# One row-maximum instruction for both heads of a softmax step, over a score tensor of two PSUM banks

## The reference, cut to what matters

```python
xn = layernorm(x)                                   # x: 8 batches x 512 rows x 256
out = x + attn(xn) + ffn(xn)
# attn: 16 heads of 16 channels, causal
score = Q @ K.T / 4 + mask
p = exp(score - max(score, axis=-1)); p = p / sum(p)
a = (p @ V) @ WO
# ffn: 16 heads of 64 channels, no mask, rotary q and k
p = softmax(q @ k.T / 8)
v = sum over the 2 chosen of 8 experts of gate * (x @ Wv[expert])
o = p @ v;  src2 = sum over the 2 chosen of 8 experts of gate * (o @ Wo[expert])
src = ln(x + src2);  ln(src + relu(src @ W1 + b1) @ W2 + b2)
```

## Time and profile before

| | |
|---|---|
| median of 3 runs | 3404.29 us (3403.39 to 3406.31) |
| span of the profiled execution | 3401.4 us |
| PE busy | 3233.1 us, 95% |
| DVE busy | 2439.7 us, 72% |
| ACT busy | 1961.5 us, 58% |
| POOL busy | 1441.9 us, 42% |
| row maxima (L1136) | 1024 instructions, 551.8 us busy |
| exponentials (L957) | 1024 instructions, 590.7 us busy |

### The profile page before, as it was taken

The page is one execution under the profiler, slowest core; times in us unless marked ns, Lnnn a source line. Parts: engine busy times, 40 slices in busy tenths (PEclk is TensorE's granted clock), DMA queues, the critical chain, the costliest instruction groups (busy, mean ns, idle before and its releaser), DMA issues.

```text
span 3401.4 us, 64468 instructions
## 1 busy us (share of the span) xinstructions
PE 3233.1 (95%) x18240; PEld 2378.9 (70%) x18240; DVE 2439.7 (72%) x4708; ACT 1961.5 (58%) x4509; POOL 1441.9 (42%) x1215
## 2 busy tenths in 40 slices
PE   1699999999999999999999999999999999997998
PEld 1577777777777777777777777777777777775765
DVE  6577777777777777777777777777777777775554
ACT  2466666656666666666666666666666666664121
POOL 4144355445443454345543554434534543442212
PEclk9999999999999999999999999999999999999999
DMA  5223333334233333233233332333332433333221
GB/s 165 76 71 87 95 90 85 77 76 109 76 84 87 84 98 81 75 100 96 69 87 76 96 98 77 76 104 81 84 87 68 114 81 75 84 75 110 72 83 62
DMA packets 115937, 295.18 MB, mean 87 GB/s; under 512 B 33856, under 2 KB 54592, under 8 KB 99264
## 3 DMA queue, kind: packets, MB, share of 16 engines
q1 hardware_dynamic: 115904, 294.78, 32.9%
HBM read 262.74 MB, written 31.98 MB: 87 GB/s over the span
## 4 chain that ended last, share of the span: by engine, by line
PE 85%; issue 6%; DVE 5%; ACT 3%; DMA 1%; POOL 0%; ACTq 0%; SPq 0%; DVEq 0%; POOLq 0%
PE bank L673 27%; PE bank L799 22%; PE bank L718 9%; PE bank L773 7%; PE bank L688 5%; PE bank L905 4%; PE bank L897 3%; PE bank L693 3%; PE bank L745 2%; PE bank L754 2%; ACT probs L957 2%; DVE uf L1239 1%; DVE oo L1232 1%; PE bank L694 1%; ACT pt_e L977 1%
## 5 line engine op out<-in xcount | busy, mean ns | idle before, releaser
L573 POOL TENSOR_TENSOR u_l<-uf,u_h 128x512 fp32r<-128x512 f32 x512 | 716.1, 1409 | 722.6 <-ACT u_h L1041 722.4
L1136 DVE TENSOR_REDUCE nmax<-bank 128x1 f32<-128x512 f32 (+3 forms) x1024 | 551.8, 579 | 305.0 <-PE bank L688 297.8
L673 PE MATMUL bank<-wv_h,xx 128*128 128x512 f32 x2048 | 755.0, 410 | 7.1 <-DVE vm L1157 7.1
L957 ACT ACTIVATE probs<-bank,nmax 128x512 f32<-128x512 f32 (+3 forms) x1024 | 590.7, 610 | 253.2 <-DVE nmax L1136 253.1
L1041 ACT ACTIVATE u_h<-uf 128x512 fp32r<-128x512 f32 x512 | 321.7, 632 | 696.9 <-DVE uf L1239 683.6
L673 PEld LDWEIGHTS bank<-wv_h,xx 128*128 128x128 f32 x2048 | 386.0, 188 | 155.8 <-issue 59.6
L718 PEld LDWEIGHTS bank<-ident_sb,probs 128*128 128x128 f32 x3328 | 388.3, 141 | 106.4 <-issue 51.3
L718 PE MATMUL bank<-ident_sb,probs 128*128 128x128 f32 x3328 | 451.3, 274 | 1.6 <-ACT stackT L1032 0.9
L569 POOL TENSOR_TENSOR v_sb<-v_next,zero_hb 128x512 f32<-128x512 f32 x64 | 74.2, 1160 | 891.9 <-PE bank L773 877.4
L799 PE MATMUL bank<-u_h,wo_h 128*128 128x512 f32 x1024 | 427.1, 417 | 5.0 <-ACT u_h L1041 3.2
L1239 DVE TENSOR_TENSOR uf<-oo,go 128x512 f32<-128x512 f32 x512 | 416.2, 823 | 8.8 <-POOL u_l L573 6.6
(11 more groups left out here) (141 smaller groups left out, 5164.2 us busy)
## 6 DMA issues: line engine op xcount, KB each, us to landing
go<-go_d SPq DMA_DIRECT2D x256, 512.0 KB, 6.5
xx<-xs_d SPq DMA_DIRECT2D x128, 512.0 KB, 3.5
oo<-scale_d SPq DMA_DIRECT2D x128, 128.0 KB, 2.9
a_d<-a_out SPq DMA_DIRECT2D x128, 128.0 KB, 2.3
pt_c<-in_x SPq DMA_DIRECT2D x16, 512.0 KB, 4.7
st<-in_wv SPq DMA_DIRECT2D x16, 512.0 KB, 5.8
st<-in_wo SPq DMA_DIRECT2D x16, 512.0 KB, 7.2
go_d<-go_turned SPq DMA_DIRECT2D x256, 8.0 KB
```

Of the source, the lines that this page charges most:

```text
L573: nc.gpsimd.tensor_tensor(u_l[:, e % 2], uf[:, e % 2], u_h.bitcast(f32)[:, e % 2], ALU.subtract).then_inc(ul_done, 1)
L673: last = nc.tensor.matmul(out, lhs, rhs, start=n == 1, stop=n == 3 * len(chunks))
L957: nc.scalar.activation(probs[:, s % 2, j, 0:w], sbank[j][:, 0:w], ACT.Exp, bias=nmax[:, 2 * s + j:2 * s + j + 1], **kw).then_inc(exp_done, 1)
L1136: nc.vector.tensor_reduce(nmax[:, 2 * s + j:2 * s + j + 1], sbank[j][:, 0:w], AX.X, ALU.max, negate=True).then_inc(nmax_ready, 1)
```

## The change

The two score banks become one tensor `score` of [128, 2, 512], that is two banks, and `sbank[j]` its halves; the other six banks are declared behind it (so the banks have other addresses, with the same use). A step's two row maxima, one for each head, become one instruction that reads both halves and writes two columns of `nmax`. It waits until the scores of both heads are complete; it raises `nmax_ready` once a step instead of twice, and ACT waits once a step, ahead of the exponential of head 0.

```diff
-        bank = [ctx.enter_context(nc.psum_tensor(f"bank{i}", [NP, S], f32)) for i in range(8)]
+        score = ctx.enter_context(nc.psum_tensor("score", [NP, 2, S], f32))
+        sbank = [score[:, j] for j in range(2)]
+        others = [ctx.enter_context(nc.psum_tensor(f"bank{i}", [NP, S], f32)) for i in range(6)]
+        bank = [o[:] for o in others[0:2]] + sbank + [o[:] for o in others[2:6]]
         ybank = bank[0:2]
-        sbank = bank[2:4]
...
                 for j in range(2):
-                    act.wait_ge(nmax_ready, n * UNITS + 2 * s + j + 1)
+                    if j == 0:
+                        act.wait_ge(nmax_ready, n * SLOTS + s + 1)
...
             def row_max(s, n):
 
                 w = S if s % 2 == 0 else (s // 2 + 1) * NP
-                for j in range(2):
-                    dve.wait_ge(s_full, n * UNITS + 2 * s + j + 1)
-                    nc.vector.tensor_reduce(nmax[:, 2 * s + j:2 * s + j + 1], sbank[j][:, 0:w], AX.X, ALU.max, negate=True).then_inc(nmax_ready, 1)
+                dve.wait_ge(s_full, n * UNITS + 2 * s + 2)
+                nc.vector.tensor_reduce(nmax[:, 2 * s:2 * s + 2], score[:, :, 0:w], AX.X, ALU.max, negate=True).then_inc(nmax_ready, 1)
```

## The result

The changed kernel takes 3459.73 us (3458.57 to 3461.42), against 3404.09 us before: 1.0161 times, 95% interval 1.0146 to 1.0175. It is slower, as forecast, and within 1 us of the forecast time. That closeness is luck: it hides three terms that were each off, one of them in its sign, and they happen to add up to the right sum. The profiled execution has a span of 3457.2 us, 55.8 more than before's.

What follows compares the result with a forecast made beforehand. PE, busy 95%, was taken as the bound, DVE counting only where PE waits. Delays of 0.37, 0.43 and 0.09 make 0.89 us a pair, x 63 = 56 us, so 3460 us, 1.65% slower; range 3431 to 3478.

Steps and rivals of the forecast that it cites:

- The estimate that the prediction made beside it: Joint 2 x 512 maximum on DVE: by the skill's 125 ns access overhead it would take 1.24 us, saving 0.125.
- Length of the instruction: Joint maximum of 2 x 512 columns on DVE: 1.22 us, between bounds of 1.216 and 1.36.
- Rival 2: The two-bank read saves nothing: joint maximum 1.36 us, exponentials 0.67 late, kernel 3482 us; chance 0.10.
- A: Step 5, maximum 6: late exponentials delay q_h and q_l, so V5's weight load starts 0.37 us later a pair.
- B: Step 7, next pair's maximum 0: late SO0 and SO1 copies hold turn(7)'s head 1 transposes, +0.43 us a pair.
- C: Step 2, maximum 3: exponentials 0.29 later delay UH2 and POOL's chain, so J3 loads +0.09 us later a pair.
- Only one of A and B: Rival: only one of the delays A and B bites, giving 3430 to 3436 us; chance 0.15.
- Faster: Rival: DVE's gain reaches PE, QK1's wait shortens by 0.07 us a pair, 3396 to 3400 us; chance 0.05.
- No change: Rival: ACT's waits take up the exponentials' delay and the gain is off the path, 3404 us; chance 0.07.

## Why the prediction was right, point by point

**The bound.** PE sets the pair and DVE's saved time counts only where PE waits for it: borne out. DVE's saving of 0.07 in a step of 512 columns is real (1.13 to 1.14 from a joint maximum's start to the next instruction's) and moved nothing at most places. The estimate that the prediction made beside it took the 0.125 of the Trainium skill, Perfetto Trace Analysis, Optimizing Scalar/DVE Operations, off the lengths of the profile's rows, while the page gives it as engine-busy time; what answers to that here is the distance from start to start, and one instruction less saved 0.07 of it.

**Length of the instruction:** 1.22 taken, 1.221 measured. Rival 2, no saving (1.36), falls with it.

**A, V5:** 0.37 forecast; 0.45 by the blocks, 0.44 by the pairs. Right mechanism, shown twice over, by the two instructions at step 6 and by the moved q_h. It was mis-sized for two small reasons. "Waiting for head 1's adds nothing" was off: the maximum starts 1.03 us after the scores' first load instead of 1.00, so that the exponentials are 0.57 late and not 0.53. And the 0.04 that QK1 came sooner is lost again at V5; against the blocks ahead of QK1 only 0.42 is lost, and that is what the 0.37 stood for.

**B, turn(7):** 0.43 forecast, 0.63 by the blocks of one pair, 0.59 by their medians and by the pairs. The mechanism was right, the sizing failed in three steps. The exponentials are 0.57 late, as in A. The prediction took a release to last 0.05, from DVE to a load; from ACT's copy to turn(7)'s load it is 0.12, so the room of 0.05 was none: the fifth load stood at SO1 already. And the lead of the loads was to take up 0 to 0.11 of the lateness; it took up nothing. By the medians from the first load of scores(0), SO1's end, head 1's first load and the load of scores(1) behind turn(7) are each 0.57 later. That head 0's four are late as well was overlooked; no run shows what it costs apart, and since head 1's are released by SO1 alone it needn't cost anything.

**C, J3:** +0.09 forecast, -0.13 measured. This is the step that failed: "The maximum ends earlier, ACT is no sooner free: 0", said of maximum 2. It is true of ACT, and what stands behind the maximum on DVE was not followed. That chain, the second half of the expert choice, leads to maximum 3, and DVE runs through it without a gap, so a start 0.07 sooner went on; across the stretch in which POOL works it even grew to 0.2. The exponentials of step 3 start 12.55 after AT's start instead of 12.49, so 0.06 later and not 0.29, and the u_h behind them comes earlier (13.28 instead of 13.42), since the uf that held it is earlier too.

**Sum:** 0.89 forecast, 0.83 by the pairs' medians, 63 of them 52 us; the other 3 or 4 of 55.8 lie outside the repeated pairs. The first copy to v_sb comes 1.3 later, and the first pair is 1.6 longer, 0.8 more than the others (but it differs by 2 between the kernels whose other pairs are like before's, so this isn't put down to the maxima). The misses of A and B (+0.05 against the blocks ahead, and +0.16) and of C (-0.22) cancel, and nothing in the prediction made them. Without that the forecast would have been some 13 us off: the kernel with two instructions at step 2, where C's 0.07 is there, takes 3473.

**Rivals.** Only one of A and B: each bites alone, and they add up. Faster: it did not come through QK1, which got 0.04, but there was a gain on the path, 7 us with the six joint maxima that do no harm; the prediction had priced such a gain at 4 to 8 and placed it wrongly. No change: it falls with the time.

## What to carry to other kernels

Merging two instructions that feed a second engine takes away the overlap of the second with the first: the consumer starts late by nearly a whole instruction (here 0.54 us) to save a tenth of one. Look for each place whether the consumer sits waiting, and how much room what is queued behind it has; merge only where the consumer is late by itself. And follow an earlier end along its own engine's queue too, not only to the consumer of its result.

## What was not expected of the hardware

- A 128x128 tensor_tensor on DVE that meets POOL's 128x512 one takes 1.39 or 1.25 us instead of 0.29 and ends 0.15 us after POOL's does, if POOL's began first; if DVE's began first, it keeps its 0.29 and POOL's takes 1.42 instead of 1.28. A shift of DVE by 0.06 decides which instruction of a chain is caught, and so moves what follows by 0.2.
- The same shows at `uf<-oo,go`, 128x512: each of those that took over 0.75 us (189 of 512 before, 313 with step 2 alone joint) began while an instruction of POOL ran and ended 0.54 to 0.55 us after its end. That is 0.40 more than the 0.15, for 384 columns more, as the maxima of 128 and 512 columns differ (0.280 and 0.681): by this estimate the columns run only once POOL is done.
- Busy time on DVE therefore holds such waits: with step 2 alone joint it rose from 2439.7 to 2549.0 us though 64 instructions are fewer, the mean of `uf<-oo,go` from 0.823 to 1.072 us, and the pair is shorter all the same.
- The time from a result to the waiting weight load differed with the place: 0.05 us from DVE's q_l to V5 (63 times), 0.12 us from ACT's copies to the transposes (62).
- A reduction over two halves in neighbouring PSUM banks runs at the rate of one bank: 1.221 us for 1024 columns, by the 1.216 that the 128- and 512-column ones give.
